# Four 256-byte piece loads per block of rows, turned by VectorE in 32x32 squares instead of by TensorE; rows of other blocks weighted zero

## The reference, cut to what matters

```python
# T = 2048 tokens, H = 256, E = 32 experts, M = 176, TOPK = 6 of E per token
combine = zeros((T, E)).at[arange(T)[:, None], topk_idx].add(topk_w)
g = einsum('th,ehm->etm', xf, gate_w)
u = einsum('th,ehm->etm', xf, up_w)
eo = einsum('etm,emh->eth', silu(g) * u, down_w)
routed = einsum('te,eth->th', combine, eo)
out = x + gb * (routed + shared)
```

## Time and profile before

| | us |
|---|---|
| median of 3 runs | 576.58 (573.74 to 577.72) |
| the profiled execution | 579.25 |
| its span, first to last instruction | 577.5 |
| TensorE matmul busy (of the span) | 477.1 (83%) |
| VectorE busy | 214.9 (37%) |
| ScalarE busy | 179.1 (31%) |
| GpSimd busy | 288.2 (50%) |

### The profile page before, as it was taken

How to read it: one execution, slowest core, us unless ns; L and a number is a source line. 1 busy time by engine, 2 the same in 40 slices (tenths; PEclk the granted TensorE clock), 3 DMA queues, 4 the chain that set the end, 5 groups by cost and what they waited for, 6 DMA issues and landing times.

```text
span 577.5 us, 9410 instructions
## 1 busy us (share of the span) xinstructions
PE 477.1 (83%) x1970; PEld 320.7 (56%) x1971; DVE 214.9 (37%) x738; ACT 179.1 (31%) x529; POOL 288.2 (50%) x257
## 2 busy tenths in 40 slices
PE   5898987984868999198999989999999998998700
PEld 4455745473525555066666657666767676665400
DVE  2726566466555211022233223223322332332137
ACT  2321323121201222033344335444434443444300
POOL 2304400278777777324555545555645556556422
PEclk9998979888597999688999989999989999999855
DMA  8999510035788964357566555657656566766376
GB/s 284 366 340 370 201 37 1 24 125 177 207 261 282 360 226 155 134 154 136 93 113 106 90 97 97 101 92 127 101 92 105 95 106 95 119 107 99 42 217 237
DMA packets 94400, 89.09 MB, mean 154 GB/s; under 512 B 22601, under 2 KB 88619, under 8 KB 94380
## 3 DMA queue, kind: packets, MB, share of 16 engines
q1 hardware_dynamic: 72492, 58.43, 34.3%
q0 software_dynamic: 19584, 28.33, 26.7%
q10 hardware_dynamic: 2304, 2.10, 1.1%
HBM read 46.88 MB, written 42.99 MB: 156 GB/s over the span
## 4 chain that ended last, share of the span: by engine, by line
DMA 28%; PE 24%; POOL 17%; issue 13%; DVE 6%; ACTq 5%; SPq 4%; ACT 3%; POOLq 1%; DVEq 0%
DMA token_sums<-tok_buf,dest 18%; POOL pair_rows L565 16%; DMA tok_buf<-pair_rows 8%; PE bank L1420 6%; PE bank L1242 4%; ACTq L367 4%; PE bank L1435 3%; PE bank L1228 3%; SPq L367 2%; ACT tok_buf L775 2%; PE bank L1144 1%; DMA XH<-in_L_attn_x 1%; PE bank L1176 1%; PE bank L1413 1%; DVE XH L1137 1%
## 5 line engine op out<-in xcount | busy, mean ns | idle before, releaser
L592 POOL DMA_INDIRECT token_sums<-tok_buf,dest x104 | 162.0, 1558 | 150.6 <-ACT tok_buf L775 70.1
L1420 PE MATMUL bank<-gate_up,tok_buf 128*128 x416 | 147.1, 477 | 10.3 <-DVE tok_buf L1093 9.9
L565 POOL DMA_INDIRECT pair_rows<-XH,rows_i x96 | 94.7, 987 | 61.3 <-DVE rows_i L1018 33.2
L1435 PE MATMUL bank<-down,tok_buf 88*128 x416 | 111.8, 392 | 0.0
L1420 PEld LDWEIGHTS bank<-gate_up,tok_buf 128*128 128x128 f32 x416 | 79.0, 195 | 47.0 <-issue 20.9
L1093 DVE COPY tok_buf<-bank 128x256 f32<-128x256 f32 x104 | 44.2, 425 | 89.1 <-PE bank L1413 87.4
L1435 PEld LDWEIGHTS bank<-down,tok_buf 88*128 88x128 f32 x416 | 72.2, 194 | 8.0 <-issue 0.3
L757 ACT ACTIVATE tok_buf<-bank 128x176 f32<-128x176 f32 x104 | 33.0, 317 | 102.4 <-PE bank L1420 58.8
L775 ACT ACTIVATE tok_buf<-bank,tok_buf 128x256 f32<-128x256 f32 x104 | 49.1, 472 | 32.5 <-PE bank L1435 32.3
L1413 PE MATMUL bank<-ident,tok_buf 128*128 128x128 f32 x208 | 42.2, 286 | 14.8 <-DMA tok_buf<-pair_rows 12.0
L1413 PEld LDWEIGHTS bank<-ident,tok_buf 128*128 128x128 f32 x208 | 28.1, 145 | 47.1 <-issue 25.2
(11 more groups left out here) (150 smaller groups left out, 415.8 us busy)
## 6 DMA issues: line engine op xcount, KB each, us to landing
tok_buf<-pair_rows SPq DMA_DIRECT2D x104, 128.0 KB, 2.9
gate_up<-in_L_ffn_gate_w SPq DMA_DIRECT2D x8, 704.0 KB, 8.5
gate_up<-in_L_ffn_up_w SPq DMA_DIRECT2D x8, 704.0 KB, 8.8
down<-in_L_ffn_down_w SPq DMA_DIRECT2D x2, 2816.0 KB
pair_rows<-sh_rows SPq DMA_DIRECT2D x1, 5120.0 KB, 18.9
gate_up<-token_sums SPq DMA_DIRECT2D x16, 256.0 KB, 5.9
tok_buf<-pair_rows SPq DMA_DIRECT2D x104, 32.0 KB, 2.3
XH<-in_L_attn_x SPq DMA_DIRECT2D x4, 512.0 KB, 9.4
```

Source lines behind the costliest of these rows:

```text
L565: nc.gpsimd.indirect_dma_start(out=pair_rows, out_offset=bass.IndirectOffsetOnAxis(ap=rows_i[:, t, k:k + 1], axis=0), in_=XH[:, t, :], in_ ...
L592: nc.gpsimd.indirect_dma_start(out=token_sums[c % 2], out_offset=bass.IndirectOffsetOnAxis(ap=dest[:, c:c + 1], axis=0), in_=yw[:, c, :], ...
L1420: last = mm(banks[1 + c % 2][:, 0:M2], xT[:, c % 2, k, :], gate_up[:, bass.ds(e * (KC * M2) + k * M2, M2)], start=k == 0, stop=k == KC - 1)
L1435: last = mm(banks[4 + c % 2][:, 0:C], aT[0:KD, c % 2, m, :], down[0:KD, bass.ds(e * C + m * E * C, C)], start=m == 0, stop=m == 1)
```

## The change

- `load_rows` issues four transfers for a block, one for each quarter q of the 256 columns (64 columns, 256 bytes). Quarter q goes to partitions 32q to 32q+31: partition 32q+b holds the four pieces of rows b, 32+b, 64+b, 96+b.
- `turn_x` moves to VectorE: one transpose instruction on 32x32 squares from `xg` to `xT`. TensorE's transposes and VectorE's copy go. Column q*64 + k*32 + a of a row lands on partition q*32 + a of half k, so the weights' rows are loaded in that order: `load_gate_up` issues four transfers of 32 partitions where it issued one.
- The slot in `xg` is free at `xT_copied`, which SP now waits for.
- `own_rows` (1 for a block's own rows, 0 for others) takes the place of `bad_rows`. `pick_weight` moves to VectorE and multiplies the scores by it; VectorE now loads the map values and ScalarE doesn't.
- `bound_tokens` and `dest` go. `scatter` takes the token number from `rec`. The cleared head rows now carry token number `T`, so they are still left out; overlapping rows are added with weight zero.

```diff
             def load_gate_up(e0, e1, s):
                 for a, w in enumerate((gate_w, up_w)):
                     for k in range(KC):
-                        sp.dma_start(gu_v[:, e0:e1, k, a * M:(a + 1) * M],
-                                     w[e0:e1, k * P:(k + 1) * P, :].rearrange("e p m -> p e m")).then_inc(s, 16)
+                        for q in range(QS):
+                            row = (q * KC + k) * S
+                            sp.dma_start(gu_v[q * S:(q + 1) * S, e0:e1, k, a * M:(a + 1) * M],
+                                         w[e0:e1, row:row + S, :].rearrange("e p m -> p e m")).then_inc(s, 16)
...
             def load_rows(c, col):
-                sp.dma_start(xg[:, c, :], pair_rows[bass.DynSlice(col, P, E), 0:C]).then_inc(x_loaded[c], 16)
+                rows = pair_rows[bass.DynSlice(col, P, E), 0:C].rearrange("(i b) (q w) -> q b i w", b=S, q=QS)
+                for q in range(QS):
+                    sp.dma_start(xg[q * S:(q + 1) * S, c, :].rearrange("b (i w) -> b i w", i=QS),
+                                 rows[q]).then_inc(x_loaded[c], 16)
...
-                        sp.wait_ge(x_turned, R * turn + c + 1)
+                        sp.wait_ge(xT_copied, R * turn + c + 1)
                         load_rows(c, cols[c + R])
...
                 pool.wait_ge(y_scaled, n + 1)
-                pool.wait_ge(dest_ready, n + 1)
                 wait(pool, scattered[(c - 2) % R], 16 * turns)
                 pool.sem_inc(pool_passed, 1)
                 nc.gpsimd.indirect_dma_start(
-                    out=token_sums[c % 2], out_offset=bass.IndirectOffsetOnAxis(ap=dest[:, c:c + 1], axis=0),
+                    out=token_sums[c % 2], out_offset=bass.IndirectOffsetOnAxis(ap=rec[:, c, E:E + 1].bitcast(i32), axis=0),
...
-            def copy_x(c, n):
-                dve.wait_ge(x_turned, n + 1)
+            def turn_x(c, n, turn):
+                dve.wait_ge(x_loaded[c], 16 * QS * (turn + 1))
                 if not isinstance(n, int) or n >= 2:
                     dve.wait_ge(gu_done, n - 1)
-                V.tensor_copy(xT[:, c % 2], banks[0][:, 0:C].rearrange("p (k n) -> p k n", k=KC)).then_inc(xT_copied, 1)
+                V.transpose(xT[:, c % 2].rearrange("p k (i b) -> p i k b", b=S), xg[:, c, :].rearrange("p (i k a) -> p i k a", i=QS, k=KC)).then_inc(xT_copied, 1)
...
-            def bound_tokens(c, turn, n):
+            def pick_weight(c, turn, n, e):
                 dve.wait_ge(rec_loaded[c], 16 * turn + 16)
-                V.tensor_tensor(dest[:, c:c + 1], rec[:, c, E:E + 1].bitcast(i32), bad_rows[:, bass.ds(n, 1)],
-                                ALU.max).then_inc(dest_ready, 1)
+                V.tensor_tensor(pair_weight[:, c:c + 1], rec[:, c, bass.ds(e, 1)], own_rows[:, bass.ds(n, 1)],
+                                ALU.mult).then_inc(weight_ready, 1)
...
             def step(turn, last):
-
+                experts = load_values(dve, D, 0, turn, 0)
                 for c in range(R):
                     n = R * turn + c
-                    if not first(n):
-                        bound_tokens((c - 1) % R, turn - (c == 0), n - 1)
                     if not last or c + 2 < R:
-                        copy_x(c, n + 2)
+                        turn_x((c + 2) % R, n + 2, turn + (c + 2) // R)
                     if not last or c + 1 < R:
                         multiply(c + 1, n + 1)
-                    if last and c == R - 1:
-                        bound_tokens(c, turn, n)
+                    pick_weight(c, turn, n, experts[c])
```

More of the change, by code:

```diff
@@ L24, in build_block @@
     GT = 4
+    S = 32
+    QS = P // S
     NG = TB // GT
@@ L97, in build_block @@
         zeros = sh_rows[:, :, :].rearrange("p s c -> p (s c)")[:, 0:XW]
-        bad_rows = sb("bad_rows", [P, P])[:, :]
-        dest = sb("dest", [P, 4], i32)
+        own_rows = sb("own_rows", [P, P])[:, :]
         rows_i = sb("rows_i", [P, NT, TOPK], i32)
@@ L199, in build_block @@
         zeros_ready, sums_clear, heads_clear = sem("zeros_ready"), sem("token_sums_clear"), sem("segment_heads_clear")
-        dest_ready = sem("destinations_ready")
         sh_stored = [sem(f"shared_rows_stored{s}") for s in range(2)]
@@ L208, in build_block @@
         scattered = [sem(f"scattered{s}") for s in range(R)]
-        x_turned, xT_copied, gu_done, silu_done, act_done, act_turned, aT_copied, y_done, y_scaled = (
-            sem(n) for n in ("x_turned", "xT_copied", "gate_up_done", "silu_done", "act_done", "act_turned", "aT_copied", "y_done", "y_scaled"))
+        xT_copied, gu_done, silu_done, act_done, act_turned, aT_copied, y_done, y_scaled = (
+            sem(n) for n in ("xT_copied", "gate_up_done", "silu_done", "act_done", "act_turned", "aT_copied", "y_done", "y_scaled"))
         OT = 2
@@ L506, in link @@
                 pool.wait_ge(pool_own, done[0])
-            nc.gpsimd.memset(sh_rows[:, :, :], 0.0).then_inc(zeros_ready, 1)
+            link(nc.gpsimd.memset(sh_rows[:, :, :], 0.0))
+            nc.gpsimd.iota(zeros[:, C + E:C + E + 1].bitcast(i32), [[0, 1]], base=T, channel_multiplier=0).then_inc(zeros_ready, 1)
             link(nc.gpsimd.memset(ident[:, :], 0.0))
@@ L764, in copy_act @@
                                      ACT.Copy).then_inc(aT_copied, 1)
-            def pick_weight(c, turn, e):
-                act_e.wait_ge(rec_loaded[c], 16 * turn + 16)
-                nc.scalar.activation(pair_weight[:, c:c + 1], rec[:, c, bass.ds(e, 1)], ACT.Copy).then_inc(weight_ready, 1)
             def weigh(c, n):
@@ L779, in _ @@
             silu(0, 0)
-            A = mybir.EngineType.Activation
             def step(turn, last):
-                experts = load_values(act_e, A, 0, turn, 0)
                 for c in range(R):
@@ L791, in step @@
                         weigh((c - 1) % R, n - 1)
-                    pick_weight(c, turn, experts[c])
                     if last and c == R - 1:
@@ L1077, in _ @@
             ps = await_result(dve, ("map",))
[L1078 to L1081, removed]
+            link(V.tensor_scalar(own_rows, ps[:, 2 * P:3 * P], iota_p[:, 0:1], None, ALU.is_le))
+            link(V.scalar_tensor_tensor(out=own_rows, in0=ps[:, 3 * P:4 * P], scalar=iota_p[:, 0:1], in1=own_rows,
+                                        op0=ALU.is_gt, op1=ALU.mult))
             V.tensor_copy(map_i[0:1, 0:2 * MAP_W].rearrange("p (a n) -> p a n", a=2)[:, :, 1:P + 1],
@@ L1099, in multiply @@
                 V.tensor_tensor(act[:, c % 2, :], act_g[:, c % 2, :], banks[1 + c % 2][:, M:M2], ALU.mult).then_inc(act_done, 1)
-            def bound_tokens(c, turn, n):
+            def pick_weight(c, turn, n, e):
                 dve.wait_ge(rec_loaded[c], 16 * turn + 16)
-                V.tensor_tensor(dest[:, c:c + 1], rec[:, c, E:E + 1].bitcast(i32), bad_rows[:, bass.ds(n, 1)],
-                                ALU.max).then_inc(dest_ready, 1)
+                V.tensor_tensor(pair_weight[:, c:c + 1], rec[:, c, bass.ds(e, 1)], own_rows[:, bass.ds(n, 1)],
+                                ALU.mult).then_inc(weight_ready, 1)
             for c in range(2):
-                copy_x(c, c)
+                turn_x(c, c, 0)
             multiply(0, 0)
+            D = mybir.EngineType.DVE
             def step(turn, last):
+                experts = load_values(dve, D, 0, turn, 0)
                 for c in range(R):
                     n = R * turn + c
-                    if not first(n):
-                        bound_tokens((c - 1) % R, turn - (c == 0), n - 1)
                     if not last or c + 2 < R:
-                        copy_x(c, n + 2)
+                        turn_x((c + 2) % R, n + 2, turn + (c + 2) // R)
                     if not last or c + 1 < R:
                         multiply(c + 1, n + 1)
-                    if last and c == R - 1:
-                        bound_tokens(c, turn, n)
+                    pick_weight(c, turn, n, experts[c])
             blocks(dve, step)
@@ L1403, in _ @@
                 pe.wait_ge(drained[bank], uses[bank])
[L1404 to L1414, removed]
+            pe.wait_ge(ld_early, 16 * EARLY // 8 * 2 * KC * QS)
+            pe.wait_ge(ld_late, 16 * (2 + 2 * KC * QS))
             def gate_and_up(c, n, e):
@@ L1441, in _ @@
             for c in range(2):
-                turn_x(c, c, 0)
-            for c in range(2):
                 gate_and_up(c, c, experts[c])
@@ L1451, in step @@
                     n = R * turn + c
-                    if not last or c + 2 < R:
-                        turn_x((c + 2) % R, n + 2, turn + (c + 2) // R)
                     turn_act(c, n)
```

## The result

The changed kernel takes 636.86 us (median of 4, 634.65 to 637.26) against 576.18 us for the kernel before in the same rounds: a ratio of 1.1082 over the rounds, 95% interval 1.1045 to 1.112 (the two medians alone give 1.105). The profiled execution has a span of 634.9 us, 57.4 more than the 577.5 before.

A forecast was written before the change was run, and what follows sets the result against it. SP's queue was taken to bound the changed loop: 579.25 (profiled execution) + 177.8 for issues - 126.5 of waits + 5 for waits left - 4 for the tail = 631.6, or 629 on the median's footing; range 590 to 665.

The forecast's parts named there:

- SP's issues decide: SP's queue in the block loop: 312 added row-load issues cost 177.8 us, hidden only by SP's 126.5 us of waits; 68%.
- The price of one, 0.57: Each added row-load issue on SP: 0.53 us including its address work, plus 0.04 for several runs per partition; bounds 0.33 and 0.65.
- The waits vanish, all but 5 us: SP's 126.5 us of waits in the block loop would go, with 5 us kept for the start and late landings.
- A turn of 13.3 us: One loop turn of four blocks: 6.5 us of SP's own work plus 12 issues at 0.57, against 11.25 us now.
- Weight loads fit in, up to 12 us at risk: Before the loop: 48 early weight issues take 25 us against 29.7; at half rate SP would be 30 us later.
- The cover of 17 us: SP's slack before the loop against slower weights: the wait of 8.03 and the time from 57.6 to the store at 67.26.
- Tail -4: Behind the last turn's map load: 4 us saved on blocks that the other engines have already worked off.
- TensorE's transposes worth nothing, VectorE's 0.43: In the loop: TensorE's floor falls to 2.27 us a block without gain behind SP; VectorE's replacement transpose takes 0.43 us.
- TensorE busy some 70%: A sign expected in the profile after the change: TensorE busy about 70% of the block loop.
- Low clock, DMA engines: In the loop: TensorE's lower clock adding 34 us, 663, had 9%; DMA engines at most 2.64 of 3.3 us a block, no bound.
- The rule weighed: The Trainium skill's statement that initiating a DMA is usually small beside it; the prediction read it as making 312 issues free.
- the first rival: Added SP issues cost at most 0.3 us each and the scatter-to-weighing wait loop shortens: 562 us; 4%.

## Why the prediction was right, point by point

*SP's issues decide.* Right, and shown from both sides: four issues of whole rows make the loss without the rest of the change, and two of the four taken off SP remove 43 us of it.

*The price of one, 0.57.* Too high: 0.50. The 0.04 for a second dimension did not appear (the transfer is 317 ns, has 0.33), and in the loop the pieces stand closer than the 0.53 of the prologue. 312 x 0.50 = 156 us, 22 less than the term.

*The waits vanish, all but 5 us.* Nearly: 1.5 us are left in the loop and 4.7 behind the last map load. But of the 126.5 us only 119.4 lay between the first and last map load; 7.1 belong to the tail, where no issue was added. Between the map loads that gives 156 - 119.4 + 1.5 = 38; measured 47.2. The remaining 9 us lie in SP's own work, which was taken as unchanged. Summed over the trace, its 27 map loads took 49.0 us instead of 46.6, 2.4 more; the transfer of a record load rose from 333 to 352 ns, 2.0 us over the loop; and the 312 pieces cost some 2 us more than 0.50 each, since a few transfers are long (up to 1032 ns). The last 3 us were not traced.

*A turn of 13.3 us.* The 25 intervals between SP's map loads inside the loop have a mean of 13.15 and a median of 12.86.

*Weight loads fit in, up to 12 us at risk.* This was the step that failed: the sum had 0 and it was 9.3, inside the risk that was named. The cover of 17 us was counted up to the store's issue. But the store then ran beside a 5 MB clearing that had moved with the weights (landing at 78.2 instead of 65.3), and VectorE waited for the store. Nor was all of the cover idle time of SP's: the "wait of 8.03" is the issue of the gate rows' store behind the clearing, and it moved with it (9.73 here, 0.31 where the clearing stands elsewhere). What would be late next had to be followed through the DMA engines, not only through SP. The late weight loads did fit in.

*Tail -4.* It was +0.9.

*TensorE's transposes worth nothing, VectorE's 0.43.* VectorE's took 0.445. That its map load costs nothing while SP binds is shown by the changed kernel with that load moved; for the transposes it is argued from the full queue. The gap near 2 us a turn was real: ahead of VectorE's transpose stand 56.4 us in which the engine waited for nothing that the profile shows ("issue"), 2.4 a turn, and TensorE waited 53.2 us for that transpose in the stretch shown.

*TensorE busy some 70%.* It was 81%. The 70% divided the 9.1 us a turn of the chain by 13.3; the busy time of a block is 243.53/94 = 2.59 us here (the ends are modelled), so the share is no measure of the chain.

*Low clock, DMA engines.* The clock is 0.94 in the loop, and the same pieces issued from two queues took 43 us less, so neither bound. The bound of 37 ns for a 256-byte piece was far off: a packet of SP's queue, most of them 256 bytes now, takes 17 ns on average, and a block's transfers cost the engines 1.4 us more (12.1 against 10.7) where the bound was 14.2.

*The sum.* Measured terms: 156 for the issues, -119.4 and +1.5 for the waits, 9 of SP's other work, 9.3 ahead of the loop, 0.9 behind it: 57 us, where the prediction had 177.8 - 126.5 + 5 - 4 = 52. That 629 came near 637 is luck in part, errors against each other: 22 too much for the price and 3.5 for the waits left stood against 9 for the weights, 9 for SP's other work, 7 for waits that belonged to the tail and 5 for the tail itself. With the price as measured the prediction's own sum gives 607, 30 us too low.

*The rule weighed.* An issue is small beside its transfer, as the Trainium skill says ("DMA: Bandwidth & Descriptors", section "Issuing engines are not separate DMA queues"): 0.50 us beside landings near 2. The trace does not bear out what the prediction drew from it, that the issues would be free: then the first rival's 562 would have come; the kernel with one piece a block, where the further issues are really gone, took 574.7 with its late start of 9 us. The same section says that a second issuing queue saves only the issue time; here that time was 43 us.

## What to carry to other kernels

Count a queue's issues per turn of the loop against the turn, including the registers for each address: when issues times price go over the queue's slack, each further one costs its full price, and whatever is gained on the engines is worth nothing. Read that price from a trace for the very shape of transfer: for 64 partitions it was well above that for 32 or 128. Where early transfers become slower or later, follow which transfer then stands behind which one up to the first engine that waits. A map load of 2 us costs by its place in the queue: put it behind the work that another engine waits for.

## What the runs showed of the hardware

- A transfer of 128 pieces of 256 bytes over 32 partitions holds SP for 317 ns, about as long as one of 128 rows of 1 KB (333 ns) or one of 32 such rows (316 ns); with its two address instructions it comes every 0.50 us. One of 64 rows of 1 KB over 64 partitions held SP for 483 ns, and two of them took 1.14 us.
- With 256-byte pieces SP's queue had 66384 packets in 94 blocks, with 1 KB rows 26492 in 92 blocks (each block has 128 records of 256 bytes besides, in both); they took the DMA engines 12.1 and 10.7 us a block, 17 and 37 ns a packet on average.
- A 2 KB store issued right behind the 5 MB clearing held SP's queue for 8.03 and 9.73 us; with the clearing elsewhere it held it for 0.31 us (59.58).
- VectorE turned 128x256 fp32 in 32x32 squares in 445 ns, from SBUF to SBUF; its copy of the same size from PSUM took 425.
- The weights' 12 early transfers over 128 partitions were issued in 29.7 us (16.67 to 46.40); as 48 over 32 partitions they took 41.8 (17.05 to 58.85), for the same bytes.
